# Issuing the addition of a tile's results ahead of the gather of later rows in the expert loop of a vision-transformer tower

## The chip, the cores and the metric

The kernel is one program on one NeuronCore of a Trainium2 chip. The metric is the device time of one execution in microseconds (us). Three executions of the kernel before took 797.53, 798.94 and 801.26 us; their median, 798.94 us, is the time before.

## What is computed

The reference is a small tower over 64 images of 64x64 pixels: 1024 tokens of 192 elements, in float32. The stages are a patch embedding of shifted images, an attention block with 12 heads, a block of attention and MLP in a large and a small branch, a differential attention, and at the end a mixture of experts. Only the last stage is touched here. Its reference, cut to what matters:

```
glog = xf @ Wg + bg;  ggates, gidx = topk_gates(glog, 2)      # 4 groups, 2 taken
elog = xf @ We + be;  egates, eidx = topk_gates(elog, 4)      # 8 experts in each, 4 taken
combine = gw[:, :, None] * ew                                 # weight of 32 experts, 8 not zero
for g in range(4):
    h = gelu(einsum('nd,edm->enm', xf, W1[g]) + b1[g])        # 192 -> 768
    o = einsum('enm,emd->end', h, W2[g]) + b2[g]              # 768 -> 192
    y = y + einsum('end,ne->nd', o, combine[:, g, :])
```

So each token goes through 8 of 32 experts, and its 8 results, weighted, are added to its row.

## The kernel before

The stages ahead of the experts run in an order written out by hand (`tower_order`, lines 57 to 84). They end with a table that sorts the chosen pairs of token and expert by expert, in tiles of 128 rows; the inputs of this case give 80 tiles, and an expert has from one to a few of them. The tokens' normalized rows, 192 elements with the 32 weights of the experts behind them, lie in memory as `normed_rows`; the sums that the results are added to lie in the output `out`.

The expert loop then runs on four engines at once. Each has its own instruction stream and its own loops over the tiles, and semaphores alone bind them. For tile i:

- GpSimd (POOL), lines 595 to 628, issues two indirect DMAs for each tile, in a loop over pairs of tiles that is written out for s = 0 and s = 1. The gather of line 616 fetches the 128 rows of tile i+4 into one of two staging buffers, `mo_stage`. The addition of line 622 adds the 128 results of tile i, from one of two buffers `mo_res`, to their rows of `out`. Ahead of them, line 610 waits until the addition of tile i-2, which used the same result buffer, has landed, and line 611 tells VectorE that this buffer is free (`result_free`). Line 612 waits until VectorE has put the row numbers for the gather in place (`fetch_set`); line 614 waits until the gather before it has landed (`rows_in`). Line 618 waits for the results (`result_ready`), and line 620 for those earlier additions that may touch the same tokens (`settled`, read from a table by line 608).
- VectorE (DVE), lines 1161 to 1194, takes in iteration i, in this order: the transposed rows of tile i+1 out of PSUM (line 1170); the copy of the gathered rows of tile i+2 out of the staging buffer, in three pieces (lines 1164 to 1166), for which the gather must have landed; the row numbers for the gather of tile i+4 (line 1186); the weighted result of tile i out of PSUM (line 1188); and, once line 611 has told that the buffer is free, the token numbers and the result into the buffer of the addition (lines 1192 and 1194).
- TensorE (PE), lines 1457 to 1489, multiplies tile i with the first weights (line 1475, 12 matmul instructions here, then line 1478), transposes the rows of tile i+1 (line 1460), and multiplies with the second weights (line 1483).
- ScalarE (ACT), lines 775 to 794, applies the gelu (line 787), and at the first tile of an expert issues the load of the expert three further on, as two DMAs of 579 and 576 KB (lines 406 and 407, called in line 780), so 28 loads in the loop; four buffers hold the weights.

Where VectorE goes from one expert to the next, it reads the tile numbers of the next expert (lines 1177 and 1178) between line 1194 and line 1170. GpSimd's two kinds of DMA are issued on one queue; the weights go through the queue of ScalarE.

Of the kernel before, what the change touches and what calls it, by code (L numbers as in the profile page):

```python
# [23 lines left out]
D = 192  # L24
# [91 lines left out]
def vit_tower(nc, a, out):  # L116
    ctx = ExitStack()
    with ctx:
        def sb(name, shape, dtype=F32):
            return ctx.enter_context(nc.sbuf_tensor(name, shape, dtype))  # L120
# [5 lines left out]
        def sem(name):  # L126
            if name not in sems:
                sems[name] = ctx.enter_context(nc.semaphore(name))
            return sems[name]
# [47 lines left out]
        number_u = sb("number_u", [P, 2], U32)  # L177
# [31 lines left out]
        def view(parts, n):  # L209
            v = arena[0:parts, at[0]:at[0] + n]  # L210
            at[0] += n
            return v
# [58 lines left out]
        mo_res = view(P, 2 * D)  # L271
# [196 lines left out]
        def _(pool):  # L468
# [116 lines left out]
            for s in range(2):  # L585
                if s:
                    pool.wait_ge(sem("accumulated0"), 16)
                pool.indirect_dma_start(out=out, out_offset=bass.IndirectOffsetOnAxis(ap=number_u[:, 0:1], axis=0),
                                        in_=padrow[:, 0:D], in_offset=None, compute_op=ALU.add).then_inc(sem(f"accumulated{s}"), 16)
# [5 lines left out]
            for n in range(4):  # L595
                if n:
                    pool.wait_ge(sem("rows_in"), 16 * n)
                if n >= STAGE:
                    pool.wait_ge(sem("rows_staged"), n - STAGE + 1)
                pool.indirect_dma_start(out=mo_stage[:, n % STAGE * ROWN:(n % STAGE + 1) * ROWN], out_offset=None, in_=normed_rows,  # L600
                                        in_offset=bass.IndirectOffsetOnAxis(ap=table_u[:, n:n + 1], axis=0)).then_inc(sem("rows_in"), 16)
            pool.wait_ge(sem("sums_begun"), 16 * T)
            pool.wait_ge(sem("landing_known"), 1)
            with pool.Fori(0, pairs) as pair:
                for s in range(2):
                    i = pair * 2 + s
                    fetch_set, fetched = pool.snap(i + 1), pool.snap(i * 16 + 64)
                    settled = pool.value_load(landed[0:1, bass.ds(i, 1)], min_val=16, max_val=8 * MAXT + 16)
                    added, result = pool.snap(pair * 16 + 16), pool.snap(i + 1)
                    pool.wait_ge(sem(f"accumulated{s}"), added)  # L610
                    pool.sem_inc(sem("result_free"), 1)
                    pool.wait_ge(sem("fetch_set"), fetch_set)
                    pool.sem_inc(sem("fetching"), 1)
                    pool.wait_ge(sem("rows_in"), fetched)
                    pool.sem_inc(sem("fetching"), 1)
                    pool.indirect_dma_start(out=mo_stage[:, s * ROWN:(s + 1) * ROWN], out_offset=None, in_=normed_rows,  # L616
                                            in_offset=bass.IndirectOffsetOnAxis(ap=fetch_u[:, s:s + 1], axis=0)).then_inc(sem("rows_in"), 16)
                    pool.wait_ge(sem("result_ready"), result)
                    pool.sem_inc(sem("adding"), 1)
                    pool.wait_ge(sem(f"accumulated{1 - s}"), settled)  # L620
                    pool.sem_inc(sem("adding"), 1)
                    pool.indirect_dma_start(out=out, out_offset=bass.IndirectOffsetOnAxis(ap=number_u[:, s:s + 1], axis=0),  # L622
                                            in_=mo_res[:, s * D:(s + 1) * D], in_offset=None, compute_op=ALU.add).then_inc(sem(f"accumulated{s}"), 16)
            for s in range(2):
                pool.wait_ge(sem(f"accumulated{s}"), pool.snap(pairs * 16 + 16))
                pool.sem_inc(sem("adding"), 1)
# [5 lines left out]
        def _(act):  # L632
# [70 lines left out]
            def attend(L, n, s):  # L703
                _, q, _ = attended(n, s)
                if q is not None:
                    ps = filled(act, L, "oT", q)
                    k = turn[L, q]
                    if k >= 2:
                        act.wait_ge(full_of(*by_turn[k - 2][:1], "proj", by_turn[k - 2][1]), uses[by_turn[k - 2][0], "proj", by_turn[k - 2][1]][1] + 1)
                    nc.scalar.activation(oT[:, k % 2, :, :].rearrange("p k x -> p (k x)"), ps[0:HC, 0:2 * P], ACT.Copy).then_inc(free_of(L, "oT", q), 1)  # L710
# [87 lines left out]
        def _(dve):  # L798
# [116 lines left out]
            def attend(L, n, s):  # L915
                res = {"A": h, "B": z}[L]
                t, _, p = attended(n, s)
                if t is not None:
                    ps = filled(dve, L, "PT", t)
                    k = turn[L, t]  # L920
                    if k >= 3:
                        dve.wait_ge(full_of(*by_turn[k - 3][:1], "oT", by_turn[k - 3][1]), uses[by_turn[k - 3][0], "oT", by_turn[k - 3][1]][1] + 1)

                    src = ps[:, 0:D].rearrange("p (h i) -> p h i", i=NTOK)
                    tt(out=ptbd[k % 3], in0=repeat(src, 2, TB),
                       in1=repeat(repeat(blockmask[:], 1, H), 3, NTOK), op=ALU.mult).then_inc(free_of(L, "PT", t), 1)
                if p is not None:
                    dve.wait_ge(sem(f"biased_{L}"), p + 1)
                    ps = filled(dve, L, "proj", p)
                    tt(out=res[:, p, :], in0=ps[:, 0:D], in1=res[:, p, :], op=ALU.add).then_inc(free_of(L, "proj", p), 1)  # L930
# [633 lines left out]
```

## Time and profile before

One more execution was run under the profiler. It took 803.63 us, of which the profile's span covers 801.8 us; the median of the three others is 798.94 us.

| engine | busy us | share of the span |
|---|---|---|
| PE (matmul) | 693.9 | 87% |
| DVE | 421.6 | 53% |
| POOL | 322.3 | 40% |
| ACT | 234.8 | 29% |

The expert loop runs from about 419 us to 795 us of the span. Each row of the profile's groups names a line of the kernel, an engine and an operation, with its busy time and what ended the idle time before it. "L616 POOL" is the gather and "L622 POOL" the addition; the busy time of such a row is the time in which GpSimd issues the DMA, not the transfer.

### The profile page before, as it was taken

To read this page: it belongs to the slowest core of one execution; us is meant where nothing else is said; L and a number is where in the kernel's file an instruction comes from. 1 tells how busy PE (TensorE), PEld (TensorE's weight loads), DVE (VectorE), ACT (ScalarE), POOL (GpSimd) and SP (SyncE) were. 2 spreads that over 40 slices of the span, in tenths; PEclk is the share of its full clock that TensorE was granted. 3 is DMA by queue.
4 is the path that set the end of the run, shared out by engine and by line. 5 is a ranking of instruction groups with operands and counts; after the bars stand their busy time and mean duration, and the time that the engine had idled before them with its cause. 6 is when DMAs were issued, how large, how long until landed. Compare 5 with 4: busy or idle time off the path is not lost.

```text
span 801.8 us, 19926 instructions
## 1 busy us (share of the span) xinstructions
PE 693.9 (87%) x6364; PEld 587.1 (73%) x6364; DVE 421.6 (53%) x1247; ACT 234.8 (29%) x671; POOL 322.3 (40%) x260
## 2 busy tenths in 40 slices
PE   5938948898989997894539989999999999999995
PEld 5714645655755785783239879999999999899995
DVE  7675573735578229975943343443444434444442
ACT  3102312123146201101414323334333343334332
POOL 6739020011033402421014355655555555465554
PEclk9957968577989899985559999999999999999998
DMA  9900000000000030014103756464545566456432
GB/s 347 242 1 3 1 3 2 2 2 2 1 1 0 2 117 3 0 54 129 43 18 101 232 141 166 108 161 112 157 109 155 121 188 179 117 110 165 108 54 37
DMA packets 35047, 70.00 MB, mean 87 GB/s; under 512 B 6354, under 2 KB 21299, under 8 KB 34995
## 3 DMA queue, kind: packets, MB, share of 16 engines
q0 software_dynamic: 15840, 17.71, 13.2%
q10 hardware_dynamic: 8064, 33.12, 12.1%
q1 hardware_dynamic: 11090, 18.43, 7.0%
q8 instruction: 38, 0.62, 0.3%
q14 instruction: 15, 0.11, 0.0%
HBM read 59.26 MB, written 9.98 MB: 86 GB/s over the span
## 4 chain that ended last, share of the span: by engine, by line
PE 67%; DVE 13%; DMA 8%; issue 7%; ACT 2%; POOL 1%; POOLq 0%; DVEq 0%; ACTq 0%; another core or an unknown queue 0%; SPq 0%
PE bank L1483 14%; PE bank L1475 10%; PE bank L1478 7%; DMA arena<-normed_rows,fetch_u 6%; PE bank L1331 4%; PE bank L1263 4%; PE bank L1367 3%; PE bank L1209 3%; PE bank L1283 3%; PE bank L1460 3%; PE bank L1347 2%; PE bank L1358 2%; DMA out_dram<-arena,number_u 1%; PE bank L1301 1%; PE bank L1274 1%
## 5 line engine op out<-in xcount | busy, mean ns | idle before, releaser
L622 POOL DMA_INDIRECT out_dram<-arena,number_u x80 | 127.1, 1588 | 42.5 <-issue 28.5
L616 POOL DMA_INDIRECT arena<-normed_rows,fetch_u x80 | 78.3, 979 | 127.5 <-DMA out_dram<-arena,number_u 49.5
L787 ACT ACTIVATE arena<-bank,arena 128x128 f32<-128x128 f32 x234 | 64.6, 375 | 115.9 <-PE bank L1478 115.9
L1170 DVE COPY arena<-bank 128x256 f32<-128x256 f32 x81 | 34.4, 424 | 118.3 <-PE bank L1460 80.5
L1483 PE MATMUL bank<-arena 128*128 128x192 f32 x468 | 83.5, 327 | 0.7 <-ACT arena L787 0.4
L1483 PEld LDWEIGHTS bank<-arena 128*128 128x128 f32 x468 | 75.3, 190 | 1.9 <-ACT arena L787 1.9
L530 POOL TENSOR_SCALAR rstd<-mv 128x4 f32<-128x4 f32 x12 | 2.7, 228 | 168.8 <-DVE mv L874 168.8
L1188 DVE TENSOR_SCALAR arena<-bank,arena 128x192 f32 x80 | 33.4, 418 | 52.1 <-PE bank L1483 45.6
L1475 PE MATMUL bank<-arena 128*128 128x128 f32 x468 | 58.8, 276 | 1.3 <-issue 0.7
L558 POOL TENSOR_TENSOR arena<-arena,v_space 128x2304 f32<-128x2304 f32 x8 | 34.5, 4318 | 62.4 <-DVE arena L1103 62.4
L787 ACT ACTIVATE arena<-bank,w_space 128x128 f32<-128x128 f32 x132 | 37.1, 373 | 73.9 <-PE bank L1478 70.7
L1475 PEld LDWEIGHTS bank<-arena 128*128 128x128 f32 x468 | 57.0, 192 | 2.1 <-issue 1.0
L787 ACT ACTIVATE arena<-bank,w2small 128x128 f32<-128x128 f32 x114 | 31.5, 375 | 57.5 <-PE bank L1478 54.2
L1483 PE MATMUL bank<-w_space,arena 128*128 128x192 f32 x264 | 47.6, 329 | 0.4 <-ACT arena L787 0.2
L1367 PEld LDWEIGHTS bank<-ident,arena 128*96 128x96 f32 x384 | 46.1, 173 | 1.2 <-issue 1.1
L1367 PE MATMUL bank<-ident,arena 128*96 128x128 f32 x384 | 46.5, 284 | 0.0
L1460 PE MATMUL bank<-ident,arena 128*128 128x128 f32 x162 | 35.7, 302 | 10.5 <-issue 10.4
L1483 PEld LDWEIGHTS bank<-w_space,arena 128*128 128x128 f32 x264 | 42.2, 190 | 2.0 <-ACT arena L787 1.6
L1483 PE MATMUL bank<-w2small,arena 128*128 128x192 f32 x228 | 40.7, 328 | 0.6 <-DVE arena L1188 0.3
L1483 PEld LDWEIGHTS bank<-w2small,arena 128*128 128x128 f32 x228 | 36.6, 190 | 1.4 <-ACT arena L787 0.8
L1478 PE MATMUL bank<-arena 64*128 64x128 f32 x468 | 36.6, 289 | 0.0
L1475 PE MATMUL bank<-arena,w_space 128*128 128x128 f32 x264 | 34.6, 283 | 0.5 <-DVE arena L1170 0.5
(239 smaller groups left out, 1260.9 us busy)
## 6 DMA issues: line engine op xcount, KB each, us to landing
arena<-in_moe_w_dram ACTq DMA_DIRECT2D x14, 579.0 KB
arena<-in_moe_w_dram ACTq DMA_DIRECT2D x14, 576.0 KB
arena<-in_xf_dram SPq DMA_DIRECT2D x8, 512.0 KB, 9.6
w_space<-in_moe_w_dram ACTq DMA_DIRECT2D x7, 579.0 KB
w2small<-in_moe_w_dram ACTq DMA_DIRECT2D x7, 579.0 KB
w_space<-in_moe_w_dram ACTq DMA_DIRECT2D x7, 576.0 KB
wab<-in_moe_w_dram ACTq DMA_DIRECT2D x7, 576.0 KB
arena<-in_w_dram SPq DMA_DIRECT2D x8, 480.0 KB, 8.9
```

The source lines that it names most:

```text
L558: nc.gpsimd.tensor_tensor(out=prodV[t % 2].rearrange("p (b a x) -> p b a x", a=H, x=HD), in0=repeat(p, 3, HD), in1=repeat(v, 2, H), op=ALU ...
L616: pool.indirect_dma_start(out=mo_stage[:, s * ROWN:(s + 1) * ROWN], out_offset=None, in_=normed_rows, in_offset=bass.IndirectOffsetOnAxis( ...
L622: pool.indirect_dma_start(out=out, out_offset=bass.IndirectOffsetOnAxis(ap=number_u[:, s:s + 1], axis=0), in_=mo_res[:, s * D:(s + 1) * D] ...
L787: nc.scalar.activation(mo_hT[:, m, :], bank[2 + m][:, 0:P], ACT.Gelu, bias=b1[:, m:m + 1]).then_inc(free[2 + m], 1)
L1170: nc.vector.tensor_copy(mo_xT.rearrange("p k t -> p (k t)"), bank[1][:, 0:2 * P]).then_inc(free[1], 1)
L1188: ts(out=mo_new[:, bass.ds(new, D)], in0=bank[0][:, 0:D], scalar1=mo_gates[:, bass.ds(gate, 1)], scalar2=None, op0=ALU.mult).then_inc(free ...
L1263: ins = mm(ps[0:HC, :], W[:, k, o * HC:(o + 1) * HC], xT[:, k, n * HALF:(n + 1) * HALF], start=(k == 0), stop=(k == 1))
L1367: ins = mm(ps[0:HC, k * P:(k + 1) * P], prodV[q % 2][:, c:c + HC], ident[:], start=(b == 0), stop=(b == H - 1))
L1460: ins = nc.tensor.transpose(bank[1][:, k * P:(k + 1) * P], mo_x[:, k * P:(k + 1) * P], ident[:])
L1475: mm(bank[2 + m][:, 0:P], w1e[:, m * P:(m + 1) * P], mo_xT[:, 0, :], start=True, stop=False)
L1478: mm(bank[2 + m][:, 0:P], w1e[r:r + REST, c:c + P], mo_xT[r:r + REST, 1, :], start=False, stop=True).then_inc(full[2 + m], 1)
L1483: ins = mm(bank[0][:, 0:D], mo_hT[:, m, :], w2e[:, m, :], start=(m == 0), stop=(m == MC - 1))
```

## The change

In each of the two copies of the loop body, the addition of tile i and its two waits move ahead of the gather of tile i+4 and its two waits. The wait for the addition of tile i-2 and the release of the result buffer stay first. Nothing else is changed, and no wait, instruction or buffer is added or taken away.

```diff
                     pool.wait_ge(sem(f"accumulated{s}"), added)
                     pool.sem_inc(sem("result_free"), 1)
+                    pool.wait_ge(sem("result_ready"), result)
+                    pool.sem_inc(sem("adding"), 1)
+                    pool.wait_ge(sem(f"accumulated{1 - s}"), settled)
+                    pool.sem_inc(sem("adding"), 1)
+                    pool.indirect_dma_start(out=out, out_offset=bass.IndirectOffsetOnAxis(ap=number_u[:, s:s + 1], axis=0),
+                                            in_=mo_res[:, s * D:(s + 1) * D], in_offset=None, compute_op=ALU.add).then_inc(sem(f"accumulated{s}"), 16)
                     pool.wait_ge(sem("fetch_set"), fetch_set)
                     pool.sem_inc(sem("fetching"), 1)
                     pool.wait_ge(sem("rows_in"), fetched)
                     pool.sem_inc(sem("fetching"), 1)
                     pool.indirect_dma_start(out=mo_stage[:, s * ROWN:(s + 1) * ROWN], out_offset=None, in_=normed_rows,
                                             in_offset=bass.IndirectOffsetOnAxis(ap=fetch_u[:, s:s + 1], axis=0)).then_inc(sem("rows_in"), 16)
-                    pool.wait_ge(sem("result_ready"), result)
-                    pool.sem_inc(sem("adding"), 1)
-                    pool.wait_ge(sem(f"accumulated{1 - s}"), settled)
-                    pool.sem_inc(sem("adding"), 1)
-                    pool.indirect_dma_start(out=out, out_offset=bass.IndirectOffsetOnAxis(ap=number_u[:, s:s + 1], axis=0),
-                                            in_=mo_res[:, s * D:(s + 1) * D], in_offset=None, compute_op=ALU.add).then_inc(sem(f"accumulated{s}"), 16)
```

## Rows read from the trace of the kernel before

**Rows 1.** Page, part 1: busy us (share of the span) xinstructions.
```profile
PE 693.9 (87%) x6364; PEld 587.1 (73%) x6364; DVE 421.6 (53%) x1247; ACT 234.8 (29%) x671; POOL 322.3 (40%) x260
```

**Rows 2.** Chain that ended last, expert loop: start us, us, what.
```profile
418.97 2.93 PE bank L1475 x12
...
503.53 1.34 PE bank L1475 x12
...
508.05 1.34 PE bank L1475 x12
```

**Rows 3.** Waits: engine line, waited for, us in total, times, longest.
```profile
POOL arena L616 <- DMA out_dram<-arena,number_u: 49.5, 15, 4.5
...
DVE number_u L1192 <- POOLq L611: 26.3, 21, 3.2
POOL arena L616 <- DMA arena<-normed_rows,fetch_u: 25.9, 11, 4.9
```

**Rows 4.** Timeline around a calm tile start: start us, us, engine, line, operation.
```profile
563.32 0.26 DVE L1194 COPY arena<-arena  x1
563.50 0.98 POOL L616 DMA_INDIRECT arena<-normed_rows,fetch_u  x1 [1.33 <-DVE fetch_u L1186]
...
566.76 1.60 PE L1475 MATMUL bank<-arena,wab 128*128 128x128 f32 x12
566.93 0.18 DVE L1164 COPY arena<-arena  x1 [0.23 <-issue]
...
567.19 0.26 DVE L1166 COPY arena<-arena 128x192 f32 x1
567.32 0.46 ACTq L407 DMA_DIRECT2D w_space<-in_moe_w_dram  x1
...
569.16 0.44 PE L1460 MATMUL bank<-ident,arena 128*128 128x128 f32 x2
```

**Rows 5.** Chain, gathers from start of issue to landing.
```profile
426.10 2.39 DMA arena<-normed_rows,fetch_u
430.36 5.33 DMA arena<-normed_rows,fetch_u
440.01 6.82 DMA arena<-normed_rows,fetch_u
447.63 4.66 DMA arena<-normed_rows,fetch_u
```

**Rows 6.** Timeline of ACT's issues of weight loads beside those gathers.
```profile
430.45 0.45 ACTq L407 DMA_DIRECT2D w_space<-in_moe_w_dram  x1
...
439.80 0.49 ACTq L407 DMA_DIRECT2D w2small<-in_moe_w_dram  x1
...
448.52 0.46 ACTq L407 DMA_DIRECT2D arena<-in_moe_w_dram  x1
```

**Rows 7.** Timeline of POOL and DVE where loads crowd.
```profile
462.06 0.26 DVE L1194 COPY arena<-arena  x1
...
466.04 0.98 POOL L616 DMA_INDIRECT arena<-normed_rows,fetch_u  x1 [2.74 <-DMA out_dram<-arena,number_u]
...
467.32 1.59 POOL L622 DMA_INDIRECT out_dram<-arena,number_u  x1 [0.30 <-issue]
...
471.67 1.59 POOL L622 DMA_INDIRECT out_dram<-arena,number_u  x1 [1.10 <-issue]
472.36 0.15 DVE L1192 COPY number_u<-table_u  x1 [1.56 <-POOLq L611]
```

**Rows 8.** Timeline of the last tile.
```profile
788.03 1.50 PE L1475 MATMUL bank<-arena 128*128 128x128 f32 x12
...
793.65 0.26 DVE L1194 COPY arena<-arena  x1
794.84 1.59 POOL L622 DMA_INDIRECT out_dram<-arena,number_u  x1 [0.62 <-DMA out_dram<-arena,number_u]
```

**Rows 9.** Chain, an addition from start of issue to landing.
```profile
662.19 3.90 DMA out_dram<-arena,number_u
```

## The prediction

> **What bounds the kernel now.** I read the page first: TensorE is busy for 87% of the span, GpSimd for 40% [rows 1]. Nothing ahead of the expert loop is touched, so the question is what ends a tile of that loop. The chain of waits in order of time answers it. In a calm stretch it is TensorE from tile to tile, and first matmuls follow each other after 508.05 - 503.53 = 4.52 us (4.53 when taken over several tiles) [rows 2]. The first tile starts at 418.97 and the last, the 80th, at 788.03 [rows 2, 8]: 369.1 us for 79 steps, where 79 x 4.53 is 357.9. So all stalls of TensorE in the loop are worth 11.2 us. That is the most that a better order on GpSimd can give. What it can take has no such bound.
>
> The waits view tells who makes the stalls. GpSimd waits 49.5 us ahead of its gathers for additions to land and 25.9 us for the gather before; VectorE waits 26.3 us in 21 places for GpSimd to release a result buffer [rows 3]. Most of that is slack in a loop bound by TensorE, and becomes a stall only where it grows past a tile's slack. The landings show when: a gather lands 2.39 us after its issue begins when nothing else moves, but 5.33 and 6.82 us after when it meets the load of an expert's weights [rows 5]. In those two cases the gather began 0.09 us before and 0.21 us after the load's second DMA was issued, and landed 5.24 and 7.03 us after that issue. One that began 0.89 us before it landed 3.77 us after it [rows 5, 6].
>
> **Part 1: the gather moves later.** Take the calm tile of [rows 4], and count from the start P = 566.76 of the tile that begins a new expert. The results of tile P-9.06 were ready at 563.32 + 0.26 = 563.58, 5.88 us after that tile's start at 557.70; the gather began at 563.50. In the new order the addition is first. It starts 0.93 us after its results (793.91 to 794.84 for the last tile [rows 8]), so at 564.51, takes 1.59 us, and the gather follows at the same 0.30 us distance that now separates a queued pair [rows 7]: 566.40, which is 2.9 us later than before. It still must be staged before TensorE transposes it: those rows are wanted in the tile that follows P, 2.40 us into it (569.16 - 566.76), so at P + 6.93; the staging takes 0.52 us (566.93 to 567.45), and some 0.3 us go to the wake-up (my allowance), so it may land until P + 6.1. Nothing meets it: 566.40 + 2.39 = P + 2.0. The 2.9 us cost nothing there, since TensorE's work on the tile at P covers them.
>
> But the load's second DMA is issued at 567.32, P + 0.56 [rows 4]. The gather used to start 3.8 us before it and now starts 0.92 us before. By the nearest row (0.89 before, landed 3.77 after) it lands at P + 4.3: still no stall, with 1.8 us left. The next one now starts at about P + 5.1, since it must wait for that landing and 0.8 us pass between landing and next gather (446.83 to 447.63 [rows 5]). Only behind its issue is the result buffer released. From the start of an issue to line 1192 behind it go 0.7 us (471.67 to 472.36 [rows 7]), and the results follow 0.46 us later, at P + 6.3 instead of P + 5.9. The addition then runs from P + 7.2 to 8.8, and the gather behind it starts at P + 9.1. Where the expert has two tiles, the next load is issued at P + 9.06 + 0.56, so this gather starts 0.5 us before it; where the addition also has to wait for its predecessor's landing (line 620), some tenths later. It lies among the three rows: landing 3.8 to 7.0 us after the load's issue, 4.3 to 7.6 into its tile, against a limit of 6.1. The stall is 0 to 1.5 us; I take the middle, 0.75. In the old order the gather that meets a load is the one wanted a whole tile (4.53 us) later. Calm stretches hold six loads that follow another load two tiles earlier (their issues of line 407 are 536.23, 544.69, 576.86, 617.34, 626.39 and 729.67 in the timeline of ACT, like those of [rows 6]). Six times 0.75 is **+4.5 us**; the bounds are 0 and 9.
>
> **Part 2: the addition moves earlier.** In the crowded stretches (the first dozen tiles and some ten around 680 us) the stalls come through the result buffers. The results of one tile were ready at 462.32, but their addition began at 467.32, behind a gather that began at 466.04 after the wait for a landing. In the new order it begins at 463.25, 4.1 us sooner. The next addition, at 471.67, follows its predecessor's landing, and VectorE waited 1.56 us for the release behind it [rows 7]. That wait disappears; the release then hangs on the gather's landing alone. It sits at a change of expert, where VectorE has little slack, so nearly all of it is a stall of TensorE that goes. But the gathers of these stretches are themselves the chain [rows 5], and land no sooner; in places they now begin up to 1.89 us (1.59 + 0.30) later. I count two such gains, one in either stretch, less a few tenths for the later gathers: **-2.5 us**. Bounds: -8 (of the 11.2 some belongs to the start of the loop) and +3 (two gathers at 1.89, less rounding).
>
> **Part 3: the end.** The last results are ready at 793.91 and their addition begins at 794.84 either way [rows 8]. An addition lands 3.90 us after its start at a quiet moment [rows 9], so at 798.7. The last gather, useless but waited for in line 627, now starts behind it, at 796.73, and lands 2.39 us later [rows 5], at 799.1; to 799.6 if it takes a little more. **+0.6 us**, between 0.4 and 0.9.
>
> **Issue cost.** The same instructions are issued in the same numbers; GpSimd's busy time stays. A late GpSimd still turns round in 0.98 + 1.59 + two gaps, under 4.53, so it doesn't become the bound. Nothing for it.
>
> **Sum.** 4.5 - 2.5 + 0.6 = +2.6 us. Against the profiled execution, 803.63, that gives 806.2. That execution lies 4.7 us above the median of the three that are timed, so on the median's scale it is 798.94 + 2.6 = **801.5 us**, +0.3%. About 0.5% (4 us) is what a measurement of this kernel can tell from no change.
>
> **A rule of the skill.** The rows show gathers near a load landing 3.77, 5.24 and 7.03 us after its issue [rows 5, 6]. The Trainium skill (DMA: Bandwidth & Descriptors, Queues, rings and completion order) says that each DMA engine takes turns between the queues that have work, and drains a whole packet of descriptors of one before it switches. A load is two DMAs; a gather that arrives in the middle of it would by that wait for one of the two and not for both. The first number fits this, the other two don't. If it held throughout, the meeting gather would land about 3.8 us after the load's issue, and part 1 would vanish.
>
> **The rivals.**
> Collision nearly everywhere (slower): the gather starts so close to each load that it meets all of them, also where experts have three tiles and in the crowded stretches. For it: on a calm tile it already starts only 0.92 us before the load, and a delay of half a microsecond carries it in. Against: there the nearest row lands 1.8 us before its limit. It decides from the point at which gathers land over 6.1 us into a tile. Price: 26 loads (28 without the first two) by half the stall above, 0.4, is 10.4, with -2.5 and +0.6 some +8.5: **807.5 us**.
> The earlier additions win (faster): the release of result buffers was the true limit, and the gather's slack suffices. For it: 26.3 us of VectorE's waits name the release. Against: the chain names gathers far more. Price: part 1 at 0, part 2 at -6.5, part 3 at +0.6: -5.9, **793 us**.
> Turns between queues: part 1 at 0, -2.5 + 0.6 = -1.9: **797 us**. It is the meeting gather served at half of a load, as in the row of 3.77.
> Nothing moves but the end (the gather's slack hides part 1, and the crowded stretches stay bound by gathers): +0.6, **799.5 us**.
>
> **How the numbers follow.** Forecast 0.36 (its own range 799 to 804.5), collision 0.33, earlier additions 0.13, turns 0.08, end alone 0.10. Slower by over 0.5% (over 802.9) takes collision with a little of the forecast's upper end, less the part of collision that stays small: 0.38. Faster by over 0.5% (under 795) takes most of the earlier additions: 0.14. Same: 0.48. The range leaves out the lower part of "earlier additions" and the far side of collision: 795 to 811.
>
> **What would show it.** In the changed kernel's timeline of a calm tile the addition starts some 0.9 us after line 1194 and the gather 1.9 us behind it; in the chain, gathers beginning 0.5 us around line 407 of the second load of a pair appear with 5 us and more, and the stall stands before line 1460 (TensorE waiting for the staged rows) in calm stretches, 536 to 552 and 617 to 635 us. VectorE's wait for line 611 shrinks in the crowded stretches. Stalls summed from tile starts come to 13 us. I am wrong if calm tiles stay at 4.53 throughout (part 1 is empty), if line 1460 waits also at loads that follow a three-tile expert (collision), or if the stretch up to 475 us gets shorter by over 4 us.

## The result, and the profile after

The changed kernel takes 824.75 us (median of 4 executions, 817.55 to 829.24), against 800.1 us for the kernel before beside it: a ratio of 1.0305, 95% interval 1.026 to 1.035. It is slower by 3%, some 24 us; I had forecast +2.6 us and a range that ended at 811. (The 800.1 us is the median of four executions of the kernel before, the three of the section on the metric and one of 805.90.)

In the changed kernel the addition is line 616 and the gather line 622. Of its page, part 1, which answers to [rows 1], and the shares of the chain of waits by engine and by line:

```profile
PE 696.7 (84%) x6364; PEld 589.2 (71%) x6364; DVE 417.4 (50%) x1247; ACT 234.5 (28%) x671; POOL 322.1 (39%) x260
...
PE 41%; DMA 22%; DVE 15%; issue 13%; POOLq 3%; POOL 3%; ACT 1%; DVEq 1%; ACTq 0%; SPq 0%
DMA arena<-normed_rows,fetch_u 17%; PE bank L1483 5%; DMA out_dram<-arena,number_u 4%; PE bank L1331 4%; PE bank L1263 4%; PE bank L1367 3%; PE bank L1209 3%; PE bank L1283 3%; PE bank L1475 3%; PE bank L1347 2%; POOLq L608 2%; POOL out_dram L616 2%; PE bank L1478 2%; PE bank L1358 1%; PE bank L1301 1%
```

No engine has more work: the counts are equal, and the busy times are those of before within 1%. But gathers make 17% of the chain, against 6% in the page of before, and TensorE's share fell from 67% to 41%. The first tile of the loop starts at 417.81 and the last at 812.95, so the 79 steps take 395.1 us where they took 369.1 [rows 2, 8]: 26.1 us more, with stalls of 37.3 us where there were 11.2. The two profiled executions, 829.24 and 803.63 us, lie 25.6 us apart, so the whole loss is in the loop. Twenty-five tiles take over 5 us, and nearly all the others 4.53. Most of the loss lies behind the crowded beginning: from the start of the 17th tile (498.84 before, 501.37 now) to that of the last, stalls were 3.8 us and are 26.2, in 19 tiles of over 5 us, and 20 loads are issued there.

Waits, where the last figures are times and longest, as in [rows 3]:

```profile
DVE arena L1164 <- DMA arena<-normed_rows,fetch_u: 110.8, 66, 4.3
...
POOL out_dram L616 <- DMA out_dram<-arena,number_u: 32.3, 30, 2.4
...
PE bank L1460 <- DVE arena L1166: 16.2, 19, 2.1
...
PE bank L1483 <- DVE arena L1188: 7.0, 20, 0.4
...
DVE number_u L1192 <- POOLq L611: 5.6, 18, 1.5
```

The same wait of VectorE for rows in the kernel before:

```profile
DVE arena L1164 <- DMA arena<-normed_rows,fetch_u: 8.9, 12, 2.4
```

VectorE now waits 110.8 us for gathered rows, where it waited 8.9. Its wait for the release of result buffers fell from 26.3 to 5.6 us, as forecast, and it bought nothing. TensorE waits for staged rows in front of its transposes (line 1460) in 19 tiles, and 0.35 us more for VectorE's scaling in front of line 1483.

The gathers themselves meet loads no more often than before. By the landing events of the two traces, 28 of the 80 gathers take over 4 us from start to landing in the changed kernel, and 28 did in the kernel before (two landings are not recorded there): as many as there are loads. What the move took away is the time that a gather had before its rows were wanted.

One such stall, from the timeline of the changed kernel:

```profile
579.82 0.26 DVE L1194 COPY arena<-arena  x1
...
581.28 1.58 POOL L616 DMA_INDIRECT out_dram<-arena,number_u  x1 [1.50 <-DMA out_dram<-arena,number_u]
...
583.03 0.46 ACTq L407 DMA_DIRECT2D w2small<-in_moe_w_dram  x1
583.17 0.98 POOL L622 DMA_INDIRECT arena<-normed_rows,fetch_u  x1 [0.30 <-issue]
...
586.99 1.50 PE L1475 MATMUL bank<-arena 128*128 128x128 f32 x12
...
589.42 0.18 DVE L1164 COPY arena<-arena  x1 [3.25 <-DMA arena<-normed_rows,fetch_u]
...
590.01 0.44 PE L1460 MATMUL bank<-ident,arena 128*128 128x128 f32 x2 [0.65 <-DVE arena L1166]
590.25 0.42 DVE L1188 TENSOR_SCALAR arena<-bank,arena 128x192 f32 x1 [0.19 <-issue]
...
590.80 2.21 PE L1483 MATMUL bank<-arena 128*128 128x192 f32 x12 [0.35 <-DVE arena L1188]
...
592.04 1.58 POOL L616 DMA_INDIRECT out_dram<-arena,number_u  x1 [1.23 <-DVE arena L1194]
592.85 1.39 PE L1475 MATMUL bank<-arena 128*128 128x128 f32 x11
```

GpSimd is idle for 1.50 us ahead of the addition, and the profile names the landing of an earlier one (line 620 of before). But the result of its own tile was ready only at 580.08, so by the usual 0.93 us it could not have started before 581.01: the earlier addition costs 0.27 us of the 1.50. The gather behind it starts 0.14 us after the load's second DMA. The rows are wanted in the tile that starts at 586.99. They can be staged only from 589.42. TensorE's transposes start 3.02 us into that tile instead of 2.3, and its second matmuls wait once more, for the scaling of the tile before, which VectorE does behind the staging. The tile takes 592.85 - 586.99 = 5.86 us, 1.33 more than 4.53: 0.72 by the late transposes, 0.35 by the second wait, and some 0.26 that no row of waits names. And the result of that scaling is late, so the next addition is, at 592.04, and the next gather behind it.

### The profile page after: what moved, and what is told of

It is laid out like the page before. It is cut to its first block, busy times and chain, and to the rows that moved or that the text cites. A ratio compares the mean times of both kernels' runs of the same rounds, so it can differ in the third digit from the quotient of the medians.

```text
span 827.4 us, 19926 instructions
## 1 busy us (share of the span) xinstructions
PE 696.7 (84%) x6364; PEld 589.2 (71%) x6364; DVE 417.4 (50%) x1247; ACT 234.5 (28%) x671; POOL 322.1 (39%) x260
## 4 chain that ended last, share of the span: by engine, by line
PE 41%; DMA 22%; DVE 15%; issue 13%; POOLq 3%; POOL 3%; ACT 1%; DVEq 1%; ACTq 0%; SPq 0%
DMA arena<-normed_rows,fetch_u 17%; PE bank L1483 5%; DMA out_dram<-arena,number_u 4%; PE bank L1331 4%; PE bank L1263 4%; PE bank L1367 3%; PE bank L1209 3%; PE bank L1283 3%; PE bank L1475 3%; PE bank L1347 2%; POOLq L608 2%; POOL out_dram L616 2%; PE bank L1478 2%; PE bank L1358 1%; PE bank L1301 1%
## 5 line engine op out<-in xcount | busy, mean ns | idle before, releaser
L1483 PE MATMUL bank<-arena 128*128 128x192 f32 x468 | 85.7, 333 | 4.4 <-DVE arena L1188 4.2
L1170 DVE COPY arena<-bank 128x256 f32<-128x256 f32 x81 | 34.4, 425 | 101.9 <-PE bank L1460 87.2
L1483 PEld LDWEIGHTS bank<-arena 128*128 128x128 f32 x468 | 76.8, 193 | 7.5 <-issue 7.0
L1164 DVE COPY arena<-arena (+1 forms) x82 | 19.2, 234 | 115.8 <-DMA arena<-normed_rows,fetch_u 110.8
L1475 PEld LDWEIGHTS bank<-arena 128*128 128x128 f32 x468 | 57.4, 192 | 1.3 <-DVE arena L1170 1.3
L1460 PE MATMUL bank<-ident,arena 128*128 128x128 f32 x162 | 35.7, 302 | 25.6 <-DVE arena L1166 16.2
L1460 PEld LDWEIGHTS bank<-ident,arena 128*128 128x128 f32 x162 | 16.3, 141 | 37.0 <-DVE arena L1166 19.8
```

Of the source, the lines that this page charges most:

```text
L1170: nc.vector.tensor_copy(mo_xT.rearrange("p k t -> p (k t)"), bank[1][:, 0:2 * P]).then_inc(free[1], 1)
L1460: ins = nc.tensor.transpose(bank[1][:, k * P:(k + 1) * P], mo_x[:, k * P:(k + 1) * P], ident[:])
L1475: mm(bank[2 + m][:, 0:P], w1e[:, m * P:(m + 1) * P], mo_xT[:, 0, :], start=True, stop=False)
L1483: ins = mm(bank[0][:, 0:D], mo_hT[:, m, :], w2e[:, m, :], start=(m == 0), stop=(m == MC - 1))
```

## The experiments

Each table row gives the median, the ratio to executions of the kernel before that were taken beside it (so equal medians can have ratios some tenths of a per cent apart), and the stalls of the loop: the time from the first tile's first matmul to the last one's, less 79 x 4.53 us. The stalls are those of one profiled execution, which lay between 3.2 us under and 5.0 us over its kernel's median, so differences of a few us between them say little.

| kernel | us | ratio (95% interval) | stalls in the loop |
|---|---|---|---|
| before (profile of before) | 798.94 | | 11.2 |
| changed | 824.75 | 1.0305 (1.026 to 1.035) | 37.3 |
| before, no loads | 791.86 | 0.9928 (0.9887 to 0.9969) | 2.0 |
| changed, no loads | 789.97 | 0.9892 (0.9828 to 0.9956) | 2.0 |
| before, gather waits for the result | 807.29 | 1.0132 (1.0069 to 1.0194) | 16.5 |
| changed, scaling before staging | 835.66 | 1.0472 (1.0395 to 1.055) | 46.9 |
| changed, four stages | 814.85 | 1.0188 (1.013 to 1.0246) | 23.1 |
| before, four stages | 798.2 | 0.9971 (0.9943 to 0.9998) | 12.0 |
| changed, load half a tile later | 823.09 | 1.0309 (1.0243 to 1.0375) | 32.7 |
| changed, load by SyncE | 823.23 | 1.0266 (1.0199 to 1.0334) | 33.6 |
| changed, four results | 820.86 | 1.0269 (1.0214 to 1.0324) | 29.7 |
| changed, four stages and results | 801.87 | 1.0057 (1.0017 to 1.0098) | 8.4 |
| before, four stages and results | 799.28 | 1.0001 (0.9968 to 1.0034) | 4.8 |
| before, four results | 800.31 | 1.004 (1.0002 to 1.0078) | 11.8 |

**Without the loads.** Does the loss need the loads of weights, or is a gather behind an addition slow by itself? The cut shows ScalarE's side; TensorE's wait for the weights is changed in the same way.

```diff
-                if e and e + AHEAD - 1 < NE:
-                    act.wait_ge(full[0], first + moe_base[0])
-                    load_expert(act, (u + AHEAD - 1) % AHEAD, e + AHEAD - 1)
-                act.wait_ge(sem(f"in_expert{u}"), 32 * (e // AHEAD + 1))
+                act.wait_ge(sem(f"in_expert{u}"), 32)
```

The old order:

> The old order without the 28 loads of weights in the expert loop (experts 5 to 32 compute with the first four experts' weights, so the loads are what is left out). Collision theory (the changed kernel loses its time because gathers, issued 2.9 us later, now meet the loads): without loads each tile takes 4.53 us, so the 11.2 us of stalls in the loop shrink to the 1.8 us of the first tile: about 790 us. Queue theory (a gather issued behind an addition is slow by itself, loads or not): the same for this kernel, about 790 us.

The new order:

> The new order without the 28 loads. Collision theory: all tiles at 4.53 us, at most 2 us above the old order without loads, about 791 us; gathers start 8.7 us into their tile and land 2.6 us later. Queue theory: the distance of about 25 us between the orders stays, so some 815 us.

Both are at 790 to 792 us, with overlapping intervals, and the whole difference between the orders is gone. The windows of the new order without loads and of the changed kernel (stretch, length, busy us of PE, PEld, DVE, ACT and POOL with counts, granted clock, DMA share, GB/s):

```profile
420.00:775.00 355.00, 355.00 (x2977) 336.11 (x2976) 148.88 (x629) 131.40 (x472) 199.40 (x156) 1.00 0.29 47
```

```profile
420.00:812.00 392.00, 365.90 (x2989) 339.14 (x2989) 150.86 (x627) 132.40 (x475) 198.93 (x155) 0.99 0.50 127
```

TensorE is idle for nothing of 355 us without loads, and for 26 of 392 us with them. GpSimd is as busy in both. So the order costs nothing by itself; it needs the loads beside it.

**The gather waits for the result, but stays first.** The old order, with one wait moved up.

```diff
+                    pool.wait_ge(sem("result_ready"), result)
+                    pool.sem_inc(sem("adding"), 1)
                     pool.wait_ge(sem("fetch_set"), fetch_set)
...
-                    pool.wait_ge(sem("result_ready"), result)
-                    pool.sem_inc(sem("adding"), 1)
```

> The old order (gather, then addition), but the wait for the results stands ahead of the gather, so the gather starts about 1 us later than before (6.8 us into its tile instead of 5.8) and hangs on the result of its tile as in the changed kernel. Collision theory: what counts is when the gather starts; 1 of the 2.9 us costs a part, and with the addition's issue out of the loop from a late gather to the next late gather lateness is worked off sooner: 803 to 810 us. Dependence theory (the gather's hanging on the result does the harm, however early it is): 820 us or more.

It took 807.29 us, +1.3%: slower than before, but far less so than the changed kernel, and inside the range expected. Its waits by row (the first two answer to [rows 3]):

```profile
POOL arena L618 <- DMA out_dram<-arena,number_u: 59.2, 21, 4.9
DVE number_u L1192 <- POOLq L611: 50.6, 42, 2.4
...
DVE arena L1164 <- DMA arena<-normed_rows,fetch_u: 14.8, 12, 2.9
```

The gather's dependence on the result and its start some 1.1 us later add little to the wait for rows (8.9 to 14.8 us). What grows is VectorE's wait for the release (26.3 to 50.6 us); I read that as the addition's being later here too. So the 110.8 us of the changed kernel need what stands in front of the gather only there: the addition's 1.58 + 0.30 us and its wait for an earlier addition. Of the two the wait is small: in 75 of the 80 tiles of the changed kernel the addition starts within 1.05 us of its result, and in the other five the waits beyond 0.95 us come to 2.9 us. The row of 32.3 us above counts idle time in which mostly the result was not there either. The time of the gather's start and the addition's issue in front of it were not varied apart in this run.

**Scaling before staging.** The new order; VectorE stages the rows and sets the row numbers at the end of its iteration.

```diff
                     take_columns(i + 1)
-                    stage_rows(i + 2)
-                    nc.vector.tensor_copy(fetch_u[...], table_u[...]).then_inc(sem("fetch_set"), 1)
...
                     nc.vector.tensor_copy(mo_res[...], mo_new[...]).then_inc(sem("result_ready"), 1)
+                    stage_rows(i + 2)
+                    nc.vector.tensor_copy(fetch_u[...], table_u[...]).then_inc(sem("fetch_set"), 1)
```

> The new order, with VectorE scaling and handing over the result of tile i before it stages the rows of tile i+2 and sets the row numbers. Collision theory in the form read from the trace (late rows hold VectorE in front of its scaling, and TensorE's second matmuls wait for that scaling, which makes a stall of 1.3 us out of 0.6): the stalls of 37 us in the loop fall to 12 to 20, so 800 to 808 us. If the rows themselves were all that TensorE waits for: no change, 825 us.

I missed: 835.66 us, slower than the changed kernel. Its timeline in a calm stretch shows why it doesn't test what it was meant to:

```profile
560.63 1.50 PE L1475 MATMUL bank<-arena,w_space 128*128 128x128 f32 x12
...
561.94 0.26 DVE L1192 COPY arena<-arena  x1
...
562.75 0.26 DVE L1166 COPY arena<-arena 128x192 f32 x1
...
563.07 0.44 PE L1460 MATMUL bank<-ident,arena 128*128 128x128 f32 x2
...
565.30 1.50 PE L1475 MATMUL bank<-arena,w_space 128*128 128x128 f32 x12
```

The staging (to 563.01) now stands behind the result of the tile before (561.94) and ends just before the transposes that want it (563.07). With nothing late at all a tile takes 4.67 us, and 63 of the 79 take 4.6 to 5; those that a late gather hits take up to 8.9. Three of these also have TensorE at the lower clock: in the windows 547.30:550.70, 595.20:598.50 and 642.90:646.30 the granted clock is 0.50 or 0.51. The edit took away the slack that it should have spared. It says that slack in front of line 1460 is dear, and nothing on what the held-up scaling costs.

**Four staging buffers.** Gathers run six tiles ahead and not four, so a landing may be some 9 us later.

```diff
-STAGE = 2
+STAGE = 4
...
-        fetch_u = sb("fetch_u", [P, 2], U32)
+        fetch_u = sb("fetch_u", [P, 4], U32)
...
-            with pool.Fori(0, pairs) as pair:
-                for s in range(2):
+            with pool.Fori(0, pool.snap(pairs // 2)) as quad:
+                for r in range(4):
+                    s, slot = r % 2, (r + 2) % 4
...
-                    fetch_set, fetched = pool.snap(i + 1), pool.snap(i * 16 + 64)
+                    fetch_set, fetched = pool.snap(i + 1), pool.snap(i * 16 + 96)
```

This and the next depths assume a number of tiles that is a multiple of four (80 here). The new order:

> The new order with four staging buffers and four columns of row numbers instead of two, and the gather of tile i+6 instead of i+4, so that every gather is wanted two tiles (9 us) later while it still meets the loads (the loop of GpSimd goes by four tiles; this case has 80). Collision theory: a landing that is 4 us late no longer matters, the stalls of 37 us in the loop fall to under 12: 793 to 801 us. A theory by which the result buffers or the issue on GpSimd hold the loop: 815 us or more.

The old order:

> The old order with four staging buffers and gathers six tiles ahead. Collision theory: of the 11.2 us of stalls those that come from rows landing late go, those that come from late additions and the release of result buffers stay: 791 to 798 us, no better than the new order with four stages.

The new order fell only to 814.85 us, where I had put 801 at most, and 815 or more for a path through the result buffers or GpSimd's issue. The old one is at 798.2, just over its range, at the edge of what can be told from before; I had expected it to be no better than the new order, and it is better by 16 us. The waits of the new order with four stages:

```profile
DVE number_u L1194 <- POOLq L613: 86.1, 57, 3.9
...
DVE arena L1166 <- DMA arena<-normed_rows,fetch_u: 4.1, 21, 0.2
```

The wait for rows is gone (110.8 to 4.1 us), and most of it stands in another place: VectorE waits 86.1 us for the release of a result buffer, where the changed kernel had 5.6. The timeline of that kernel at such a place:

```profile
525.92 0.98 POOL L624 DMA_INDIRECT arena<-normed_rows,fetch_u  x1 [0.30 <-issue]
...
528.92 1.60 PE L1477 MATMUL bank<-arena 128*128 128x128 f32 x12
...
529.90 0.42 DVE L1190 TENSOR_SCALAR arena<-bank,arena 128x192 f32 x1 [0.23 <-issue]
...
532.84 0.97 POOL L624 DMA_INDIRECT arena<-normed_rows,fetch_u  x1 [3.83 <-DMA arena<-normed_rows,fetch_u]
533.67 0.15 DVE L1194 COPY number_u<-table_u  x1 [3.35 <-POOLq L613]
...
534.33 0.42 DVE L1172 COPY arena<-bank 128x256 f32<-128x256 f32 x1 [0.23 <-issue]
...
534.80 1.60 PE L1477 MATMUL bank<-arena 128*128 128x128 f32 x12 [1.09 <-DVE arena L1172]
```

There is a second path, which the prediction lacked. GpSimd tells of a free result buffer at the head of its iteration, and in its order that stands behind the gather before, which waits for the gather before it to land. The gather of 525.92 lands late, so the next starts only at 532.84. The release follows it, VectorE, which had its scaled result from 530.32, can hand it over only at 533.67 after waiting 3.35 us, takes the transposed rows behind that, and TensorE waits 1.09 us for them: the tile of 528.92 takes 5.88 us. The buffer itself had been free since 530.69, when by its landing event the addition that used it before had landed.

**When the load starts.** The new order; SyncE issues the loads, behind the first tile's transposes (some 2.3 us later) or, as a control of the change of queue, at the same point as ScalarE did.

```diff
+            sp.wait_ge(sem("table_ready"), 1)
+            for e in range(1, NE - AHEAD + 1):
+                first = expert_start(sp, e, 1)
+                sp.wait_ge(full[1], first + (moe_base[1] + 2))
+                load_expert(sp, (e - 1) % AHEAD, e + AHEAD - 1)
...
-                if e and e + AHEAD - 1 < NE:
-                    act.wait_ge(full[0], first + moe_base[0])
-                    load_expert(act, (u + AHEAD - 1) % AHEAD, e + AHEAD - 1)
```

> The new order, the loads of weights issued by SyncE instead of ScalarE, when the transposes of the expert's first tile are done, some 2.2 us later in the tile than now. Collision theory: the gather that starts 0.4 us ahead of the tile lands before the load's traffic begins, and the one that meets the load is wanted a tile later: most stalls go, 800 to 808 us. If the mere presence of loads on the path, in whatever phase, makes the loss: 820 us or more.

The control, which waits for `full[0]` and `first + (moe_base[0] + 0)` instead:

> The control of the run with later loads: the new order, loads issued by SyncE at the same event as ScalarE did (the second matmuls of the tile before are done). Both theories: as the changed kernel, 820 to 830 us; if it is much faster, the issuing queue and not the phase matters.

They took 823.09 and 823.23 us. The control came as expected; the later load should have brought at least 15 us and brought nothing. But its chain is another one. The shares of its chain by line, and one stretch of it (start us, us):

```profile
DMA out_dram<-arena,number_u 16%; DMA arena<-normed_rows,fetch_u 7%; PE bank L1484 4%; PE bank L1332 4%; PE bank L1264 4%; PE bank L1368 3%; PE bank L1284 3%; PE bank L1210 3%; PE bank L1476 3%; POOL out_dram L621 2%; PE bank L1348 2%; PE bank L1479 2%; PE bank L1359 1%; POOLq L613 1%; PE bank L1302 1%
```

```profile
576.37 7.72 DMA out_dram<-arena,number_u
...
586.81 4.96 DMA arena<-normed_rows,fetch_u
```

In the changed kernel gathers are 17% of the chain and additions 4%, in the control 15% and 6%; with the later load it is 7% and 16%. The gather that is wanted first is out of the load's way, but the addition is now in it. The one of 576.37 starts 0.56 us before the load's second DMA (576.93) and lands 7.72 us after its start. The next addition waits for it until 584.92, where its result had been ready at 579.71, and the gather behind that one starts at 586.81, 13.0 us after its tile's start, where an undisturbed one starts 8.7 us after it. Its predecessor's landing alone (584.26 by the landing event, and 0.8 us to the next start) would have let it start at some 585.1. Counted as above, the additions' waits for earlier ones come to 56 us in 32 tiles here, and to 2.9 us in five in the changed kernel. So the phase decides which of the two DMAs on the path meets the load, and in the new order the next gather is late either way: it stands behind its own predecessor and behind the additions. I had looked at gathers alone.

**Four result buffers, and both depths.** With four result buffers the release runs two tiles ahead.

```diff
-        number_u = sb("number_u", [P, 2], U32)
+        number_u = sb("number_u", [P, 4], U32)
...
-        mo_res = view(P, 2 * D)
+        mo_res = view(P, 4 * D)
...
+            pool.sem_inc(sem("result_free"), 2)
```

In the new order, alone:

> The new order with four result buffers instead of two, so that VectorE may hand over a result two tiles before the buffer's release would now let it (GpSimd's loop goes by four tiles). Collision theory with two paths (a gather that a load delays holds up the staging of its rows, and in GpSimd's instruction order also the release of the next result buffer): the second path goes, the first stays: of the 37 us of stalls 20 to 30 remain, 808 to 818 us. If the release were the whole path: 790 to 797 us. If it plays no part beside the staging: 825 us.

With four stages:

> The new order with both: four staging buffers with gathers six tiles ahead, and four result buffers. Collision theory with two paths: both are gone, nearly all tiles take 4.53 us, 788 to 796 us. With four stages alone 23 us of stalls remained; if a third path holds them, over 805 us.

In the old order, with four stages, and alone:

> The old order with both, the version that should beat both kernels: stalls of 11 us fall under 3: 788 to 794 us, and equal to the new order with both, since with slack on both paths the order of the two DMAs plays no part.

> The old order with four result buffers alone. The stalls of the old kernel in its crowded stretches come through the release of result buffers (26 us of waits of VectorE for it) as well as through gathers: 792 to 797 us. If gathers alone make them: no change, 799 us.

All four came out slower than I expected, by 2.9 to 5.9 us over the upper ends (for four result buffers in the old order the other theory, 799 us, is the one that fits). But the new order shows the two paths cleanly. Its stalls are 37.3 us as it is, 29.7 with the results alone, 23.1 with the stages alone, 8.4 with both. The two alone take away 7.6 + 14.2 = 21.8 us, together they take away 28.9: while one path stands it gives part of the gain back. The medians say the same, with 3.9 and 9.9 us alone and 22.9 together. The waits tell the same. With four results alone:

```profile
DVE arena L1167 <- DMA arena<-normed_rows,fetch_u: 111.5, 66, 3.7
```

With both:

```profile
POOL arena L625 <- DMA arena<-normed_rows,fetch_u: 50.3, 22, 4.1
...
DVE number_u L1195 <- POOLq L614: 1.6, 3, 0.6
```

And the windows of the loop with both, in which TensorE's busy time falls short of the stretch by 2.6 us, and not by 26:

```profile
425.00:783.00 358.00, 355.40 (x2960) 335.27 (x2959) 146.78 (x623) 130.78 (x469) 196.66 (x154) 1.00 0.55 138
```

GpSimd still waits 50.3 us for landings, but VectorE waits only 1.6 us for its releases. In the old order the same buffers bring nothing that can be told from before: ratios of 0.9971, 1.004 and, with both, 1.0001. With both the profiled loop was 6.5 us shorter (362.6 against 369.1 us) and the median wasn't. The two profiled executions are not typical: that of before, 803.63 us, lies 4.7 us over its median, and that of the deep version, 796.11, lies 3.2 us under. What differs between executions of one kernel, one profile each can't show, so that stays open. The two orders with both depths, expected to be equal, are 2.6 us apart (ratios of 1.0057 and 1.0001, with overlapping intervals). No version that loads all the weights beats before by an amount that I would claim.

## Why the prediction was wrong

I had named the right mechanism for the loss: a gather that starts later meets a load with less time left. What failed is part 1, above all its count of hits (six in calm stretches, where there were 19 stalls behind the first 16 tiles), then the size of a hit; part 2 failed too. The forecast of +2.6 us said in effect that nothing changes, and +24 was measured.

- *What bounds the loop.* Right: 11.2 us could be won, and what could be lost had no such bound.
- *Part 1, the shift.* Right where nothing meets the gather. In the changed kernel, near the end of the loop:

```profile
814.04 0.26 DVE L1194 COPY arena<-arena  x1
...
815.26 1.58 POOL L616 DMA_INDIRECT out_dram<-arena,number_u  x1 [1.70 <-DMA arena<-normed_rows,fetch_u]
...
817.15 0.98 POOL L622 DMA_INDIRECT arena<-normed_rows,fetch_u  x1 [0.30 <-issue]
```

The addition begins 0.96 us after its result is ready (0.93 forecast), the gather 1.89 us behind it. The landing of a gather that meets a load was well bounded too. Most of the late ones in the chain land 4.7 to 7.5 us after their start, where the rows had shown 4.66 to 6.82:

```profile
583.17 5.87 DMA arena<-normed_rows,fetch_u
...
651.92 7.50 DMA arena<-normed_rows,fetch_u
```

- *Part 1, the stall of one hit.* Failed: "0 to 1.5 us; I take the middle, 0.75". It is 1.33 us in the tile shown above (5.86 - 4.53), and 1.4 on average over the 19 tiles (26.2 / 19). That is within the bounds and nearly twice the term. I counted only the transposes' lateness, which there is some 0.7 us. Behind the staging in VectorE's order stands the scaling of the tile before, so TensorE waits a second time, 0.35 us in front of line 1483 (7.0 us in 20 places), and starts the next thing late.
- *Part 1, the count.* Failed, and this is the larger part: "Six times 0.75". Twenty-five tiles are over 5 us, and the chain has 24 gathers of 4.29 to 7.50 us, from 427.97 to 765.96, where that of before has six of over 4 us. I followed one gather from a clean start to the next load, and took a load behind an expert of three tiles for one that meets a clean start again ("still no stall, with 1.8 us left"). Here is such a case in the changed kernel:

```profile
514.60 0.98 POOL L622 DMA_INDIRECT arena<-normed_rows,fetch_u  x1 [0.30 <-issue]
...
515.52 0.46 ACTq L407 DMA_DIRECT2D w_space<-in_moe_w_dram  x1
...
520.72 0.98 POOL L622 DMA_INDIRECT arena<-normed_rows,fetch_u  x1 [1.87 <-DMA arena<-normed_rows,fetch_u]
...
524.80 0.98 POOL L622 DMA_INDIRECT arena<-normed_rows,fetch_u  x1 [0.30 <-issue]
...
528.71 0.98 POOL L622 DMA_INDIRECT arena<-normed_rows,fetch_u  x1 [0.30 <-issue]
...
529.10 0.46 ACTq L407 DMA_DIRECT2D w2small<-in_moe_w_dram  x1
```

  The first gather starts 0.92 us before the load's second DMA, as forecast, and makes no stall. But by the chain it lands 5.34 us after its start, 4.42 after that DMA, where I had taken 3.77 from the one row near it. The next gathers follow after 6.12, 4.08 and 3.91 us. A tile takes 4.53, so each of the last two makes up only 0.45 to 0.62 us. "A late GpSimd still turns round in 0.98 + 1.59 + two gaps, under 4.53" left out the way through VectorE: the release stands behind one gather, the handing over behind the release, the addition behind that, and the next gather behind the addition. At the next load, three tiles on, the gather therefore starts 0.39 us before it and not 0.92, lands 6.58 us after its start, and makes a stall: the tile of 533.06 takes 6.04 us. The other gathers that start 0.3 to 0.5 us before a load's second DMA land 6.29 to 7.50 us after their start, those that start 0.9 before it 4.68 to 5.34. So a load that follows an expert of three tiles is hit as well. Another is the gather of 765.96, beside a load issued at 766.37; it lands 6.95 us later, and the tile that starts at 770.33 lasts to 776.71. The wait of the addition for an earlier one (line 620 of before), which I had put at "some tenths later", was no more than that in the changed kernel: 0.27 us at 581.28.
- *The second path.* Missing: a gather's late landing also holds up the release of a result buffer. I wrote that "the release then hangs on the gather's landing alone" and priced it as a gain. In the changed kernel the path is hidden behind the first one (5.6 us of waits); with four stages it comes out at 86.1 us.
- *Part 2.* Wrong: the -2.5 us didn't come. From the first tile's start to the twelfth's it is 55.4 us, where it was 56.2. VectorE's wait for the release did fall by 20.7 us, but the waits for rows rose by 101.9. A wait that ends sooner gives nothing when the one beside it ends later.
- *Part 3.* Right within what can be read: from the last tile's start to the span's end there were 13.8 us and are 14.4; +0.6 was forecast.
- *The rivals.* "Collision nearly everywhere" was what happened; I gave it 0.33 and a price of 8.5 us, by "half the stall above, 0.4". At the measured 1.33 us, 26 loads would have made 35 us, so its price was too low by the size of a hit, and its chance by the error in the count. Turns between queues would have had the gathers that meet a load land at about 3.8 us after the load's issue. The gather of 583.17 (0.14 us after the issue, landing 6.0 us after it) and most of the 24 do not. They don't bear out that rule of the Trainium skill (DMA: Bandwidth & Descriptors, Queues, rings and completion order) as I had used it: it speaks of packets, and that a gather waits for one whole DMA of the two was my own step. When within the load they were served wasn't measured.

What is shown: the loads are needed (the loss is gone without them), and it goes through two paths, each of which must be deepened. What is read from rows, and not tested by itself: that lateness carried from tile to tile makes the hits so many, and how much of the loss is the later start of the gather as such and how much the longer way round by the addition's issue. The additions' waits for earlier ones are not part of it (2.9 us in five tiles), but take the gathers' place as soon as the load is moved onto the addition.

## What to carry to other kernels

When a DMA is moved in an engine's order, hold its slack against the worst landing, with the largest transfer in flight, and count in front of it every wait of what it is moved behind; then ask who waits for the signals that stand behind its own wait. Where a late landing makes the next issue late, a hit can't be priced from a clean start: work out how much a late turn makes up before the next large transfer comes. Deeper buffers help only if every path that the late landing feeds is deepened: here either depth alone left 23 to 30 of 37 us of stalls, both left 8.

## What I had not expected of the hardware

A stall can cost more than itself. In one place of the changed kernel a gather landed so late that TensorE waited 2.11 us in front of its transposes; the matmuls behind them took 3.89 us instead of 2.12:

```profile
487.78 0.44 PE L1460 MATMUL bank<-ident,arena 128*128 128x128 f32 x2 [2.11 <-DVE arena L1166]
...
488.58 3.89 PE L1483 MATMUL bank<-arena 128*128 128x192 f32 x12 [0.36 <-DVE arena L1188]
```

The windows view of that stretch (clock in the third figure from the end) shows the granted clock at 0.57, so mostly at the 1.2 GHz level:

```profile
488.50:492.50 4.00, 3.92 (x14) 3.93 (x15) 1.47 (x7) 0.00 (x0) 2.29 (x3) 0.57 0.21 35
```

That one tile took 8.97 us. Over the whole loop the clock is 0.99, so this is a small part of the loss. It doesn't follow every long wait: behind the next longest, 1.76 us at 660.38, the same 12 matmuls took 2.22 us.
